# Batch attention's output projection as rounded passes over pairs of steps, with copies moved to ScalarE

## The reference

```
q = (h @ Wq).reshape(L, B, 16, 64)
k, v = split(h @ Wkv)
score = einsum('ibnd,jbnd->ijbn', q, k) / 8
prob = softmax(score, axis=1)
vec = einsum('ijbn,jbnd->ibnd', prob, v).reshape(L, B, 1024)
x = x + vec @ Wo            # Wo: 1024 x 128
```

## Time and profile before

| | |
|---|---|
| median of 3 runs | 754.14 us (753.21 to 755.10) |
| the profiled execution's own time | 753.48 us |
| its span | 751.7 us |
| batch attention, first projection to last result copy | 460.49 to 629.6 us |
| TensorE busy | 633.7 us, 84% |
| TensorE weight loads busy | 452.9 us, 60% |
| VectorE busy | 461.1 us, 61% |
| ScalarE busy | 376.1 us, 50% |
| GpSimd busy | 266.1 us, 35% |
| output projection (line 1461), 256 records | 32.8 us busy |

### The profile page before, as it was taken

How to read it: one execution, slowest core, us unless ns; L and a number is a source line. 1 busy time by engine, 2 the same in 40 slices (tenths; PEclk the granted TensorE clock), 3 DMA queues, 4 the chain that set the end, 5 groups by cost and what they waited for, 6 DMA issues and landing times. The chain is left out here.

```text
span 751.7 us, 17224 instructions
## 1 busy us (share of the span) xinstructions
PE 633.7 (84%) x6475; PEld 452.9 (60%) x6475; DVE 461.1 (61%) x1246; ACT 376.1 (50%) x815; POOL 266.1 (35%) x369
## 2 busy tenths in 40 slices
PE   3999999899999845188999968989999996775865
PEld 2466666566666534147999925667778784342554
DVE  3565755688888749642444434666656564465895
ACT  6568676777777421144444365453444423323342
POOL 4233233444534105751545560222213130144641
PEclk9999999999999965557999987999999998796899
DMA  3032355342122210143666442000000000000001
GB/s 105 2 94 66 73 138 136 98 106 57 45 69 67 71 48 30 50 163 111 220 216 227 137 113 88 3 1 2 2 2 2 2 2 2 0 1 0 15 14 29
DMA packets 53024, 48.97 MB, mean 65 GB/s; under 512 B 10219, under 2 KB 45533, under 8 KB 52685
## 3 DMA queue, kind: packets, MB, share of 16 engines
q1 hardware_dynamic: 47933, 41.94, 18.6%
q0 software_dynamic: 2496, 4.27, 1.8%
q10 hardware_dynamic: 2512, 1.65, 0.9%
HBM read 18.68 MB, written 15.54 MB: 46 GB/s over the span
## 5 line engine op out<-in xcount | busy, mean ns | idle before, releaser
L581 ACT ACTIVATE ptx<-bank 128x512 f32<-128x512 f32 x128 | 66.0, 603 | 68.4 <-PE bank L493 68.4
L1587 POOL COPY ptx<-over_pt 32x512 f32<-32x512 f32 x64 | 38.9, 608 | 130.9 <-DVE over_pt L1557 128.1
L1151 POOL DMA_INDIRECT results<-moe_y,moe_dest x46 | 45.2, 983 | 55.8 <-DVE moe_y L1289 48.8
L393 POOL TENSOR_TENSOR x<-x,l_back 128x128 f32<-128x128 f32 x32 | 14.5, 454 | 109.5 <-ACT l_back L594 94.0
L736 DVE SCALAR_TENSOR_TENSOR ptx<-ptx,bank 128x512 f32<-128x512 f32 x64 | 41.1, 684 | 17.6 <-PE bank L503 16.2
L721 DVE TENSOR_REDUCE l_m<-bank 128x4 f32<-128x512 f32 x64 | 40.9, 678 | 15.3 <-PE bank L477 15.3
L1487 ACT ACTIVATE ke<-bank 64x512 f32<-64x512 f32 x64 | 37.9, 592 | 16.4 <-PE bank L1418 15.6
L1146 POOL DMA_INDIRECT slots<-xs,moe_pos x32 | 33.8, 1058 | 28.6 <-DVE moe_pos L1232 18.6
L721 DVE TENSOR_REDUCE l_m_raw<-bank 128x4 f32<-128x512 f32 x64 | 40.7, 673 | 0.5 <-PE bank L477 0.5
L1461 PE MATMUL bank<-over_ot,over_wo 128*128 128x128 f32 x256 | 32.8, 281 | 6.1 <-DVE over_ot L1563 6.1
L489 PE MATMUL bank<-ke 32*128 32x512 f32 x256 | 36.5, 639 | 1.1 <-DVE l_m L721 1.1
(11 more groups left out here) (354 smaller groups left out, 1664.3 us busy)
## 6 DMA issues: line engine op xcount, KB each, us to landing
slots<-blank SPq DMA_DIRECT2D x16, 528.0 KB, 4.7
ptx<-w SPq DMA_DIRECT2D x12, 578.0 KB, 3.3
ke<-w SPq DMA_DIRECT2D x11, 578.0 KB, 3.3
w<-in_w SPq DMA_DIRECT2D x16, 256.0 KB
moe_xb<-slots SPq DMA_DIRECT2D x23, 132.0 KB
x<-in_x SPq DMA_DIRECT2D x4, 256.0 KB, 4.5
w<-results SPq DMA_DIRECT2D x4, 256.0 KB, 6.0
w<-results ACTq DMA_DIRECT2D x4, 256.0 KB, 5.9
```

Of the source, the lines that this page charges most:

```text
L581: nc.scalar.activation(probs[t % 2][:, g, :], score_bank[g][:, :], ACT.Exp, scale=SCALE0).then_inc(s["probs"], 1)
L1151: nc.gpsimd.indirect_dma_start(M.results, bass.IndirectOffsetOnAxis(dest[j % 4][:, n:n + 1], 0), y[j % 4][:, n, :], None, bounds_check=2 * ...
L1587: nc.gpsimd.tensor_copy(ptx[t % 2][r, :, r], pt[t % 2][r, :, :]).then_inc(s["spread"], 1)
```

## The change

The output projection is made for two steps at once (u = a pair of steps, 256 columns). The weights `wo` are split once into `wo_hi` (by ScalarE, at its program's start) and `wo_lo` (by VectorE, after `normalise(0)`). The weighted values are split in each step into `ot_hi`, which ScalarE copies out of both `o_bank` with rounding, and `ot_lo`, which VectorE makes as the bank minus `ot_hi`. `result(u, half)` has four of the eight head pairs, with three passes for each: 12 passes in a step, 24 for a pair of steps. It runs in the steps 5 to 20: in those that are multiples of 4 before the scores (in 8 and 12 behind the group's projections), in the others where `result` stood. ScalarE copies both halves of the values and the first query block of a group. The mask operand `rows` is stored once and read 16 times, and `top`, `sums`, `inv` and `side` lie in a tensor of an earlier stage, `head_ones`.

Of the diff, lines of context are mostly left out, and every line is moved 8 columns to the left.

```diff
-s = semaphores(nc, "over", """masks ring_ps q ke v0 v1 s_ps top less exps sums inv scaled turned spread
-    o_ps o0 o1 y_ps y cosine""")
+s = semaphores(nc, "over", """masks ring_ps q q_first ke v s_ps top less exps sums inv scaled turned spread
+    o_ps o_hi o_lo y_ps y cosine wo_hi wo_lo""")
...
-hi, lo, wo, ke, ptx, yt = M.over_hi, M.over_lo, M.over_wo, M.ke, M.ptx, M.yt_all
+hi, lo, ke, ptx, yt = M.over_hi, M.over_lo, M.ke, M.ptx, M.yt_all
...
-ot = two("ot", [128, PAIR, S])
-top, sums, inv = sb("top", [S, H, 1]), sb("sums", [S, H, 1]), sb("inv", [S, H, 1])
-side, rows = sb("side", [128, S], BF16), sb("rows", [128, H, 32], BF16)
+wo_hi, wo_lo = sb("wo_hi", [128, PAIR, D], F32R), sb("wo_lo", [128, PAIR, D], F32R)
+ot_hi, ot_lo = [[sb(f"ot_{part}{n}", [128, PAIR, 2, S], F32R) for n in range(2)] for part in ("hi", "lo")]
+top, sums, inv = [M.head_ones[:, n:n + H].rearrange("p (h a) -> p h a", a=1) for n in (64, 64 + H, 64 + 2 * H)]
+side, rows = M.head_ones[:, 0:64].bitcast(BF16), sb("rows", [128, 1, 32], BF16)
...
 for t in range(G):
     if t % 4 == 0:
...
-            USES += [("q", t // 4 * PAIR + r + 1), ("ke", 2 * (t // 4 * PAIR + r + 1))]
-    USES += [("v0", t + 1), ("v1", t + 1)]
+            USES += [("q", t // 4 * (PAIR - 1) + r) if r else ("q_first", t // 4 + 1), ("ke", 2 * (t // 4 * PAIR + r + 1))]
+    USES += [("v", 2 * t + 1), ("v", 2 * t + 2)]
...
             if t == 0:
...
-            wait(pe, s["q"], t // 4, per=PAIR, plus=PAIR)
+            wait(pe, s["q_first"], t // 4, plus=1)
+            wait(pe, s["q"], t // 4, per=PAIR - 1, plus=PAIR - 1)
...
-            nc.tensor.matmul(o[:, :], side[:, :], rows[:, :, :], start=True, stop=False, skip_group_check=True)
+            nc.tensor.matmul(o[:, :], side[:, :], rows[:, :, :].broadcast_to([128, H, 32]), start=True, stop=False, skip_group_check=True)
...
         def values(t):
...
-            pe.wait_ge(s["v0"], t + 1)
-            pe.wait_ge(s["v1"], t + 1)
-            wait(pe, s["o0"], t)
-            wait(pe, s["o1"], t)
+            wait(pe, s["v"], t, per=2, plus=2)
+            wait(pe, s["o_lo"], t, per=2)
...
-        def result(t):
-            pe.wait_ge(s["o0"], t + 1)
-            pe.wait_ge(s["o1"], t + 1)
-            wait(pe, s["y"], t)
-            for r in range(PAIR):
-                mm = nc.tensor.matmul(y_bank[:, 0:S], wo[:, r, :], ot[t % 2][:, r, :], start=r == 0, stop=r == PAIR - 1)
-            mm.then_inc(s["y_ps"], 1)
-        for t in range(G + 3):
+        def result(u, half):
+            if u == 0 and half == 0:
+                pe.wait_ge(s["wo_lo"], 1)
+            if half == 0:
+                wait(pe, s["o_lo"], u, per=4, plus=4)
+                wait(pe, s["y"], u)
+            o = y_bank[:, 0:2 * S]
+            for r in range(4 * half, 4 * half + 4):
+                nc.tensor.matmul(o, wo_hi[:, r, :], ot_hi[u % 2][:, r, :, :], start=r == 0, stop=False)
+                nc.tensor.matmul(o, wo_hi[:, r, :], ot_lo[u % 2][:, r, :, :], start=False, stop=False)
+                mm = nc.tensor.matmul(o, wo_lo[:, r, :], ot_hi[u % 2][:, r, :, :], start=False, stop=r == PAIR - 1)
+            if half:
+                mm.then_inc(s["y_ps"], 1)
+        for t in range(G + 5):
...
+            if t >= 5 and t % 4 == 0:
+                result((t - 5) // 2, (t - 5) % 2)
             if t < G:
...
-            if 0 <= t - 3:
-                result(t - 3)
+            if t >= 5 and t % 4:
+                result((t - 5) // 2, (t - 5) % 2)
...
     @block.scalar
     def _(act):
+        def first_query(t):
+            act.wait_ge(s["ring_ps"], at_block(t, 0, 0) + 1)
+            wait(act, s["s_ps"], t)
+            nc.scalar.activation(q[:, 0, :], ring[at_block(t, 0, 0) % 3][:, :], ACT.Copy).then_inc(s["q_first"], 1)
...
         def values(t):
-            act.wait_ge(s["ring_ps"], at_value(t, 1) + 1)
...
-            nc.scalar.activation(v[t % 3][:, 1, :], ring[at_value(t, 1) % 3][:, :], ACT.Copy).then_inc(s["v1"], 1)
+            for half in range(2):
+                act.wait_ge(s["ring_ps"], at_value(t, half) + 1)
+                nc.scalar.activation(v[t % 3][:, half, :], ring[at_value(t, half) % 3][:, :], ACT.Copy).then_inc(s["v"], 1)
...
         def weighted(t):
...
-            wait(act, s["y_ps"], t, plus=-1)
-            nc.scalar.activation(ot[t % 2][:, 4:8, :], o_bank[1][:, :].rearrange("p (r q) -> p r q", r=4), ACT.Copy).then_inc(s["o1"], 1)
-        def result(t):
-            act.wait_ge(s["y_ps"], t + 1)
-            nc.scalar.activation(yt[:, 8 * t:8 * t + 8, :], y_bank[:, 0:S].rearrange("p (s i) -> p s i", i=B),
+            wait(act, s["y_ps"], t // 2, plus=-1)
+            for n in range(2):
+                nc.scalar.activation(ot_hi[t // 2 % 2][:, 4 * n:4 * n + 4, t % 2, :], o_bank[n][:, :].rearrange("p (r q) -> p r q", r=4),
+                                     ACT.Copy).then_inc(s["o_hi"], 1)
+        def result(u):
+            act.wait_ge(s["y_ps"], u + 1)
+            nc.scalar.activation(yt[:, 16 * u:16 * u + 16, :], y_bank[:, 0:2 * S].rearrange("p (s i) -> p s i", i=B),
...
-        for t in range(G + 3):
+        nc.scalar.activation(wo_hi[:, :, :], M.over_wo[:, :, :], ACT.Copy).then_inc(s["wo_hi"], 1)
+        for t in range(G + 5):
             if t < G and t % 4 == 0:
+                first_query(t)
...
             if t < G:
...
-            if 0 <= t - 3:
-                result(t - 3)
+            if t >= 6 and t % 2 == 0:
+                result((t - 6) // 2)
...
             if 0 <= t - 2 < G:
...
-        act.wait_ge(s["y"], G)
+        act.wait_ge(s["y"], G // 2)
...
-        def values(t):
-            dve.wait_ge(s["ring_ps"], at_value(t, 0) + 1)
-            wait(dve, s["o_ps"], t, plus=-2)
-            nc.vector.tensor_copy(v[t % 3][:, 0, :], ring[at_value(t, 0) % 3][:, :]).then_inc(s["v0"], 1)
...
         def weighted(t):
-            dve.wait_ge(s["o_ps"], t + 1)
-            wait(dve, s["y_ps"], t, plus=-1)
-            nc.vector.tensor_copy(ot[t % 2][:, 0:4, :], o_bank[0][:, :].rearrange("p (r q) -> p r q", r=4)).then_inc(s["o0"], 1)
+            wait(dve, s["y_ps"], t // 2, plus=-1)
+            for n in range(2):
+                dve.wait_ge(s["o_hi"], 2 * t + n + 1)
+                part = slice(4 * n, 4 * n + 4)
+                nc.vector.tensor_tensor(ot_lo[t // 2 % 2][:, part, t % 2, :], o_bank[n][:, :].rearrange("p (r q) -> p r q", r=4),
+                                        ot_hi[t // 2 % 2][:, part, t % 2, :].bitcast(F32), ALU.subtract).then_inc(s["o_lo"], 1)
...
-        nc.vector.tensor_scalar(rows[:, :, :], M.over_rowf[:, :].rearrange("p (a k) -> p a k", a=1).broadcast_to([128, H, 32]),
-                                -BIG, None, ALU.mult).then_inc(s["masks"], 1)
+        nc.vector.tensor_scalar(rows[:, 0, :], M.over_rowf[:, :], -BIG, None, ALU.mult).then_inc(s["masks"], 1)
         for t in range(G + 3):
             if t < G and t % 4 == 0:
-                for r in range(PAIR):
+                for r in range(1, PAIR):
...
             if t < G:
...
-                values(t)
...
+            if t == 0:
+                dve.wait_ge(s["wo_hi"], 1)
+                nc.vector.tensor_tensor(wo_lo[:, :, :], M.over_wo[:, :, :], wo_hi[:, :, :].bitcast(F32), ALU.subtract).then_inc(s["wo_lo"], 1)
```

## The result

The changed kernel took 744.97 us (median of 4 runs, 743.75 to 747.55) where the kernel before took 753.67 (4 runs, 752.98 to 755.10): a ratio of 0.9876, with an interval from 0.9854 to 0.9897, or 8.7 us less. The forecast was 746.0, from 743.8 to 751.3.

The account below looks back on a forecast made before the run. TensorE was taken to bound most stage steps, VectorE steps 0 to 3; -3.24 - 5.43 + 0.2 - 0.4 + 0.8 = -8.1 us took the median from 754.14 to 746.0 us, range 743.8 to 751.3.

Parts of the forecast that it names:

- 1. nine steps: Steps 5 to 7, 9 to 11, 13 to 15: 12 passes at 0.121 us, 1.45 where 1.81 was; -3.24 us.
- 2. steps 4, 8, 12: Group starts: no projection behind the scores; at 8 and 12 the half fits the 1.55 us key wait; -5.43 us.
- 3. ScalarE's copies at groups 8, 12: ScalarE's added copies make the first key copy 0.1 us later at steps 8 and 12; +0.2 us.
- 5. steps 0 to 3: Stage's head: VectorE delayed by low weights and second subtraction, yet first key copy at 498.4, not 498.79; -0.4 us.
- 6. the tail: After the last steps: chain of values, rounding and subtractions, 4.01 us a step, 15.2 against 14.67; +0.8 us.
- rival B: Projection passes are bound by their weight load, 0.188 us each, so the kernel is slower: +2.5, 756.6 us; chance 0.07.
- the page's rule: Skill page: same-row-group loads don't overlap matmuls, so a pass takes 216 ns; +7.9, 762.0 us; chance 0.02 within 0.07.
- Rival A: VectorE's loop exceeds TensorE's 6.26 us step, so the nine steps give nothing: -4.9, 749.2 us; chance 0.10.
- C: Rounded passes of 256 columns no cheaper than f32, near 0.17 us: 754 us; chance 0.06, including mixtures near no change.
- VectorE (4): VectorE's loop in the steps grows by two subtractions from 4.44 to 5.68 us, staying under TensorE's 6.26; no one waits.

Follow-up runs that it names:

- e4: Changed kernel with pairs, places, copies and subtractions kept, but one plain float32 product in place of three rounded passes: 747.74 us (ratio 0.9901).
- e1: Changed kernel with the halves of the projection in steps 8 and 12 put back behind the scores: 746.62 us (ratio 0.9892).
- e5: Changed kernel with the first query block of a group copied by VectorE again: 752.01 us (ratio 0.9940).
- e3: Changed kernel with two of the three passes left out, so 4 passes in a half and not 12: 738.22 us (ratio 0.9769).
- e11: The changed kernel unedited, run and profiled again (its second profile) beside a version with filled waits, early low part and plain tail: 746.10 us (ratio 0.9857).
- e2: Changed kernel with each 256-column pass split into two of 128, weights loaded again, 24 passes in a half: 767.50 us (ratio 1.0152).

## Why the prediction was right, and where its terms were off

| step of the prediction | forecast | measured |
|---|---|---|
| 1. nine steps | -3.24 | -3.33 (6.62 to 6.25) |
| 2. steps 4, 8, 12 | -5.43 | -5.37 (6.61 to 4.82) |
| 3. ScalarE's copies at groups 8, 12 | +0.2 | -0.04 |
| 5. steps 0 to 3 | -0.4 | -1.0 (34.16 to 33.18), or +0.1 with a visible fall of the clock |
| 6. the tail | +0.8 | +1.0 |
| sum | -8.1 | -8.7 in the stage (153.35 to 144.63), -7.6 with a visible fall; the medians differ by 8.7 |

The profiled execution differs by -5.9: -8.7, the 1.65 of its late start and the 1.1 of the clock. So the mechanism held term by term, but some of the closeness is luck: the head gave 0.6 us more than forecast and the group's start 0.24, the tail cost 0.2 more, and the forecast knew of neither the clock nor a scatter of whole times as large as these misses.

**The passes (1).** 0.121 us was taken and 0.120 measured, and the range's argument, that loads overlap in this kernel whatever their record says, held, and rival B, which needed the opposite, is refuted by the same number. (Its sum for the page's rule, 156 x 0.216 - 27.1, is +6.6 before the tail and not the 7.9 given; nothing hangs on it.) Rival A's condition did not come either: VectorE's loop stayed 0.6 us below TensorE's step. Nor did C's: e4 shows rounding worth about half of what was saved behind s4. But the half lasts 1.54 us, not 1.45, and the step is right all the same. The first rounded pass behind the small products takes 0.1 us more than the next ones. Before the change the value projections paid that behind the plain float32 products (the record of 0.48 at 526.82 is 0.39 now), so it only changed its owner.

**The group's start (2, 3).** Right in place: half a pair in the wait for the keys costs nothing, and e1 prices it at 1.4 us a group. The 0.2 was mis-sized, and its reason overlooked: before the change ScalarE waited 0.99 us for TensorE's first block of keys there, and the two roundings (0.97 us together; I had spaced the copies by 0.57) and the query (0.61) fit into what its one copy and that wait took. I had costed the moved query as a burden on ScalarE only; e5 shows that leaving it with VectorE, behind the new wait, costs 3.0 us in all. The prediction never priced that.

**VectorE (4).** 5.68 us was forecast for its loop and e3 shows 5.65 when it is the bound. In the change it catches up with TensorE inside a group: it doesn't wait for ScalarE's rounding at the end of its step 4, waits 0.56 us at the end of step 6 and 0.50 at the end of step 7, and nobody waits for it between step 4 and the tail.

**The head (5).** Mis-sized by 0.6 us on the good side, since ScalarE's copies follow one another faster than I took: from its exponentials to the first key copy it is 2.93 us in the second profile (494.99 to 497.92), where I had 3.43. The clock I had left out altogether. It costs at most the 1.1 us seen here, and nothing where the long values are hidden.

**The tail (6).** One link is 4.15 us, where 4.01 was forecast: 2.02 to the rounding, 0.70 to the subtractions (0.63), 1.29 for both, 0.14 to the next values (0.06). Three times 0.14 turns the 15.2 us to the start of the last copy into 15.6 (15.59 measured); rounding up to +0.8 had covered a part of it.

## What to carry to other kernels

Splitting a float32 product into three rounded ones pays only with enough columns for each weight load. Here with 128 columns the kernel was 1.5% slower than before (0.6% of it a lowered clock in that profile's tail), and with 256, got by pairing two steps, 1.2% faster. Put such work where its engine waits for another anyway, and look at every copy by what is queued behind it: who makes the first query's copy, once a group, decided 3.0 us. At the end of a stage, where nothing fills the waits, the shortest chain wins over the cheapest instruction: 0.8 us in this stage, though not shown in the whole time. And read an edit in the stretch where it acts, since whole times can scatter by more than it gives.

## What the runs showed of the hardware that was not expected

- Passes with a new 128 x 128 weight load each come 0.11 us apart with 128 columns at the full clock, 0.12 with 256 columns of float32r and 0.23 with 512. The load's own record says 0.19 us in all three, and 0.33 at the lower clock (e2's tail).
- The granted clock can fall to its lower level where TensorE waits 1.7 and 1.9 us in an otherwise busy stretch, and need not: it did in seven of ten profiles with unfilled waits, and e5 had the same two waits without it. 32 value products then take up to 3.63 us instead of 1.97, also when the group is not the first one behind the wait (e11: three passes lie between).
- ScalarE's roundings of 512 columns out of PSUM start 0.49 us apart back to back, though each record is 0.60.
